# Moving the int8-style quantisation passes of a BitLinear feed-forward from VectorE to ScalarE, with shorter and split scale chains

## The reference

```python
def act_quant(x):
    scale = 127.0 / clip(max(abs(x), axis=-1), 1e-05)
    return clip(round(x * scale), -128, 127) / scale
def bitlinear(x, w, b):                       # weights ternary, w = q * s
    return einsum('bsd,fd->bsf', act_quant(rmsnorm(x)), weight_quant(w)) + b
h = layernorm(x) * (1 + cb) + sb
x = x + gb * bitlinear(gelu(bitlinear(h, w1, b1)), w2, b2)   # 1024 -> 4096 -> 1024
```

## Time and profile before

| | |
|---|---|
| time, median of 3 runs | 6217.45 us (6212.48 to 6218.86) |
| profiled execution, time | 6216.62 us |
| its span, slowest core | 6215.1 us (cores 6200.4 to 6215.1) |
| busy: PE, DVE, ACT | 2608.1, 3996.5, 1913.1 us |
| mean granted TensorE clock | 0.685 |

### The profile page before, as it was taken

One profiled execution on the slowest core, in us unless ns is written; L12 is line 12 of the kernel. 1 busy time (PEld: TensorE's weight loads), 2 busy tenths in 40 slices (PEclk: granted clock), 3 DMA queues, 4 the chain that ended last, 5 costly groups with the idle time before them and its releaser, 6 DMA issues.

```text
span 6215.1 us, 49470 instructions; the slowest of 8 cores (6200.4 to 6215.1 us)
## 1 busy us (share of the span) xinstructions
PE 2608.1 (42%) x12096; PEld 1374.9 (22%) x12096; DVE 3996.5 (64%) x9950; ACT 1913.1 (31%) x3579; POOL 26.2 (0%) x53
## 2 busy tenths in 40 slices
PE   5612342333333234233333323200057777777777
PEld 5501221221122122122112212100023333323333
DVE  0027557566656755756665675478887777777775
ACT  0004345335334434533533443300022222222222
POOL 0000000000000000000000000010000000000000
PEclk9995565665665566566566556555578888888888
DMA  2130000000000000000000000240000000000000
GB/s 86 78 80 1 14 14 1 14 14 1 14 14 14 1 14 14 1 14 14 1 14 14 14 0 7 58 70 0 0 7 21 21 21 21 21 21 21 21 21 14
DMA packets 31716, 123.15 MB, mean 20 GB/s; under 512 B 4756, under 2 KB 6565, under 8 KB 29382
## 3 DMA queue, kind: packets, MB, share of 16 engines
q1 hardware_dynamic: 24486, 98.95, 4.5%
q0 software_dynamic: 6944, 21.05, 2.1%
HBM read 106.95 MB, written 34.08 MB: 23 GB/s over the span
## 4 chain that ended last, share of the span: by engine, by line
DVE 47%; PE 16%; DVEq 11%; DMA 7%; ACT 7%; issue 7%; ACTq 3%; SPq 1%; POOL 0%; POOLq 0%
PE psY L41 8%; DVEq L324 7%; DVE are_bf L1012 6%; DVE zz L875 5%; PE psZ L41 4%; DVE aim_bf L1018 4%; ACTq L324 3%; PE psMC L41 3%; DVE nbuf L979 2%; ACT sin_bf L988 2%; DVE bnst L1477 2%; DMA x_sb<-xmid 2%; DVE aim_bf L1003 2%; DVE wstage L1536 2%; DMA wmstg<-wmod 1%
## 5 line engine op out<-in xcount | busy, mean ns | idle before, releaser
L41 PE MATMUL psZ<-pw_sb,sel_sb 32*128 32x256 f32 x256 | 146.6, 686 | 1322.3 <-DVEq L324 852.1
L41 PE MATMUL psY<-w1q,q1f 128*128 128x512 bf16 x2048 | 566.2, 427 | 1.9 <-ACTq L324 1.7
L41 PE MATMUL psY<-w2q,q2f 128*128 128x512 bf16 x2048 | 460.3, 380 | 2.9 <-ACTq L324 2.9
L41 PE MATMUL psZ<-hbf,win 128*128 128x256 bf16 (+1 forms) x2176 | 309.7, 303 | 241.6 <-ACTq L324 239.4
L41 PE MATMUL psY<-are_bf,bd_sb 128*128 128x256 bf16 x512 | 130.8, 409 | 654.1 <-ACTq L324 644.2
L1012 DVE TENSOR_TENSOR_SCAN are_bf<-are_bf,ncar_re 128x256 bf16<-128x256 bf16 x512 | 374.5, 731 | 16.4 <-issue 1.4
L41 PEld LDWEIGHTS psZ<-pw_sb,sel_sb 32*128 32x128 f32 x256 | 66.2, 309 | 1380.5 <-issue 1377.5
L1018 DVE TENSOR_TENSOR_SCAN aim_bf<-aim_bf,ncar_im 128x256 bf16<-128x256 bf16 x512 | 371.2, 725 | 0.0
L1000 DVE TENSOR_TENSOR are_bf<-cos_bf,g_bf 128x256 bf16<-128x256 bf16 x512 | 146.1, 285 | 294.8 <-ACTq L324 278.6
L875 DVE SCALAR_TENSOR_TENSOR zz<-z,wcv_sb,zz 128x256 f32<-128x256 f32 (+1 forms) x816 | 326.7, 478 | 5.9
L1457 ACT ACTIVATE h_act<-psY,al 128x512 bf16<-128x512 f32 x256 | 175.9, 687 | 491.5 <-PE psY L41 357.7
(11 more groups left out here) (222 smaller groups left out, 5630.4 us busy)
## 6 DMA issues: line engine op xcount, KB each, us to landing
wmstg<-wmod SPq DMA_DIRECT2D x8, 3072.0 KB, 11.1
x_sb<-x SPq DMA_DIRECT2D x32, 512.0 KB, 5.9
xmid<-xo_sb SPq DMA_DIRECT2D x32, 512.0 KB, 3.2
x_sb<-xmid SPq DMA_DIRECT2D x32, 512.0 KB, 4.0
out<-xo_sb SPq DMA_DIRECT2D x32, 512.0 KB, 2.9
w1q<-w1T POOLq DMA_DIRECT2D x8, 1024.0 KB, 24.0
w2q<-w2T POOLq DMA_DIRECT2D x32, 256.0 KB, 5.7
win<-in_proj_w POOLq DMA_DIRECT2D x8, 520.0 KB, 6.2
```

Of the source, the lines that this page charges most:

```text
L41: r = _a(*args, **kw)
```

## The change

The q1 and q2h passes go from DVE to ACT, as two `activation` calls of the function Copy each, with the scale and the magic constant as scale and bias; the copy to f32 in q2h goes away. The quantisation scale is now 127 / max directly, without the inverse square root, so it can be had before qrsqrt. cs1 becomes **cs1b**, behind q1 in the program and with the qrsqrt that stood at the end of h2. st2 and cs2 become **cs2a** (four one-column operations, before q2h) and **cs2b** (the rest, behind q2h in the program, with four one-column operations in place of nine after the qrsqrt).

```diff
@@ front @@
-                    qrsqrt(e, c2, 8, 6)
+                    e.tensor_scalar(out=col(c2, 10), in0=col(c2, 7),
+                                    scalar1=1e-6, scalar2=None, op0=ALU.max)
+                    e.drain()
+                    e.reciprocal(out=col(c2, 10), in_=col(c2, 10))
+                    e.drain()
+                    e.tensor_scalar(out=col(c2, 11), in0=col(c2, 10),
+                                    scalar1=127.0, scalar2=None, op0=ALU.mult)
                 b.stage("vector", s_h2, ...
-                def s_cs1(e, c2=c2):
+                def s_q1(e, c2=c2):
+                    e.activation(out=h2_sb[:], in_=h2_sb[:], func=AF.Copy,
+                                 scale=col(c2, 11), bias=MAGIC)
+                    e.drain()
+                    e.activation(out=q1_bf[:], in_=h2_sb[:], func=AF.Copy,
+                                 bias=-MAGIC)
+                b.stage("scalar", s_q1, reads=("h2", cn),
+                        writes=("q1", "h2"))
+                def s_cs1b(e, c2=c2):
+                    qrsqrt(e, c2, 8, 6)
                     e.tensor_tensor(out=col(c2, 9), in0=col(c2, 7),
                                     in1=col(c2, 8), op=ALU.mult)
...
+                    e.tensor_scalar(out=al1[u8][:, 0:1], in0=col(c2, 9),
+                                    scalar1=col(smallc, 0),
+                                    scalar2=1.0 / 127.0, ...)
+                    e.reciprocal(out=col(c2, 14), in_=al1[u8][:, 0:1])
+                b.stage("vector", s_cs1b, reads=(cn, "smallc"),
+                        writes=(cn, f"al1_{u8}", f"iac1{up}"))
-                def s_q1(e, c2=c2, up=up):
-                    e.tensor_scalar(...); e.tensor_scalar(...)
-                b.stage("vector", s_q1, reads=("h2", cn),
-                        writes=("q1", "h2"))
@@ back @@
-                b.stage("vector", s_st2, reads=("bnst2", "amx"), writes=(cn,))
-                b.stage("vector", s_cs2, reads=(cn, "smallc"),
-                        writes=(cn, f"al2_{u8}", f"iac2{up}"))
+                b.stage("vector", s_cs2a, reads=("amx",), writes=(cn,))
                 for hh in range(8):
                     def s_q2h(e, c2=c2, hh=hh):
-                        e.tensor_copy(out=wstage[:], in_=h_act[:, hs:hs + 512])
+                        e.activation(out=wstage[:], in_=h_act[:, hs:hs + 512],
+                                     func=AF.Copy, scale=col(c2, 11),
+                                     bias=MAGIC)
                         e.drain()
-                        e.tensor_scalar(... col(c2, 11), MAGIC, mult, add)
-                        e.drain()
-                        e.tensor_scalar(out=h_act[:, hs:hs + 512], ... subtract)
-                    b.stage("vector", s_q2h, reads=(f"ha{hh}", cn),
+                        e.activation(out=h_act[:, hs:hs + 512], in_=wstage[:],
+                                     func=AF.Copy, bias=-MAGIC)
+                    b.stage("scalar", s_q2h, reads=(f"ha{hh}", cn),
                             writes=(f"ha{hh}", "wstage"))
+                def s_cs2b(e, c2=c2):      # bn_aggr, mean square, qrsqrt, al2, iacol2
+                b.stage("vector", s_cs2b, reads=(cn, "smallc", "bnst2"),
+                        writes=(cn, f"al2_{u8}", f"iac2{up}"))
```

More of the change, by code:

```diff
@@ L1375, in s_cs1 @@
                     e.drain()
-                    e.tensor_scalar(out=col(c2, 9), in0=col(c2, 9),
-                                    scalar1=1e-5, scalar2=None, op0=ALU.max)
+                    e.tensor_scalar(out=al1[u8][:, 0:1], in0=col(c2, 9),
+                                    scalar1=col(smallc, 0),
+                                    scalar2=1.0 / 127.0,
+                                    op0=ALU.mult, op1=ALU.mult)
                     e.drain()
-                    e.reciprocal(out=col(c2, 10), in_=col(c2, 9))
@@ L1483, in p2_back, with s_cs2a, s_q2h @@
                             writes=("bnst2", "amx"))
-                def s_st2(e, c2=c2):
+                def s_cs2a(e, c2=c2):
                     e.reduce_max(out=col(c2, 7), in_=amx[:, 0:8], axis=AX)
+                    e.drain()
+                    e.tensor_scalar(out=col(c2, 10), in0=col(c2, 7),
+                                    scalar1=1e-6, scalar2=None, op0=ALU.max)
+                    e.drain()
+                    e.reciprocal(out=col(c2, 10), in_=col(c2, 10))
+                    e.drain()
+                    e.tensor_scalar(out=col(c2, 11), in0=col(c2, 10),
+                                    scalar1=127.0, scalar2=None, op0=ALU.mult)
+                b.stage("vector", s_cs2a, reads=("amx",), writes=(cn,))
+                for hh in range(8):
+                    def s_q2h(e, c2=c2, hh=hh):
+                        hs = hh * 512
+                        e.activation(out=wstage[:], in_=h_act[:, hs:hs + 512],
+                                     func=AF.Copy, scale=col(c2, 11),
+                                     bias=MAGIC)
+                        e.drain()
+                        e.activation(out=h_act[:, hs:hs + 512], in_=wstage[:],
+                                     func=AF.Copy, bias=-MAGIC)
+                    b.stage("scalar", s_q2h, reads=(f"ha{hh}", cn),
+                            writes=(f"ha{hh}", "wstage"))
+                def s_cs2b(e, c2=c2):
                     e.bn_aggr(out=c2[:, 17:19], in_=bnst2[:, 0:48])
@@ L1504, in s_cs2 @@
                     e.drain()
-                    e.tensor_scalar(out=col(c2, 9), in0=col(c2, 9),
-                                    scalar1=1e-5, scalar2=None, op0=ALU.max)
+                    e.tensor_scalar(out=al2[u8][:, 0:1], in0=col(c2, 9),
+                                    scalar1=col(smallc, 2),
+                                    scalar2=1.0 / 127.0,
+                                    op0=ALU.mult, op1=ALU.mult)
                     e.drain()
-                    e.reciprocal(out=col(c2, 10), in_=col(c2, 9))
@@ L1509, in s_cs2 @@
[L1509 to L1525, removed]
+                    e.reciprocal(out=col(c2, 14), in_=al2[u8][:, 0:1])
                     e.drain()
                     e.tensor_copy(out=iacol2[up][:], in_=col(c2, 14))
-                b.stage("vector", s_cs2, reads=(cn, "smallc"),
+                b.stage("vector", s_cs2b, reads=(cn, "smallc", "bnst2"),
@@ L1529, in p2_back @@
                         writes=(cn, f"al2_{u8}", f"iac2{up}"))
-                for hh in range(8):
-                    def s_q2h(e, c2=c2, hh=hh):
-                        hs = hh * 512
-                        e.tensor_copy(out=wstage[:], in_=h_act[:, hs:hs + 512])
[L1535 to L1542, removed]
-                    b.stage("vector", s_q2h, reads=(f"ha{hh}", cn),
-                            writes=(f"ha{hh}", "wstage"))
```

13 lines of the change are left out of this document (removed).

## The result

The kernel after takes 6481.16 us (6478.02 to 6485.77), the kernel before, on the same chip, 6217.3 (6212.48 to 6219.41). The ratio is 1.0425, with an interval of 1.0414 to 1.0437. The forecast was 6494, with a range of 6360 to 6570. The profiled execution took 6483.32 us with a span of 6481.4 on its slowest core.

The account below looks back on a forecast made before the run. DVE's 49.4 us and a wait bound the kernel before; after, the chain from C (end of a unit's last w1mm) to w2mm_0. Terms +11, -2.5, +232, +20.4, +9.1, +6.9 make +277 on 6215.1, with 1.5 around it 6494 us; range 6360 to 6570.

Parts of the forecast that it names:

- DVE does not bound the cycle after: Phase 2 unit cycle: DVE, with 33 us left, bounds nothing by its sum; the chain C to w2mm_0 remains.
- The sign given for it: Profile after: DVE busy under 3.5 ms would show the forecast right.
- The 16.5 us: DVE work removed per unit: q2h 13.2 us, q1 1.65, and seven one-column operations of 0.23 each.
- cs2b behind the last q2h: On DVE, cs2b starts only after the last q2h, as it writes c2; its column reaches ia2t at C+26.0.
- The order of stages: Planner's order: ACT runs q2h 0, tq1e, q2h 1 to 7, q1, ia2e; DVE runs ln2 before stats 5 to 7.
- the rival: Second rival, DVE behind C: ln2 does not delay the stats, cs2a 4.2 us earlier for 29 cycles, 6372 us; 8 in 100.
- q2h on ACT: Between cs2a and cs2b: eight q2h take 12.3 us, 1.54 each; bounds 8.3 and 12.8.
- w2mm_0 at a low clock: Start of w2mm_0 on PE: 8.67 us in place of 7.07, 1.6 more; 0 to 3.2 possible.
- The sum: Whole run, C(u) ending unit u's last w1mm: 27 cycles at +8.6, other terms, together +277 on 6215.1.
- The start: Ahead of C(0), unit 0's last w1mm end: h2(1) and ln2(2) slip between weight reductions on DVE, +11 us.
- The first one: Freed engine sets the pace: cycle falls to PE's sum, about 5840 us, if w2mm_0 starts before C+22.7; 5 in 100.
- The third rival: On DVE, h2(u+3) goes between ln2 and stats 6, delaying cs2a 7.7 us for 28 cycles, about 6710; 7 in 100.

Follow-up runs that it names:

- e1: Kernel after with q1 and q2h put back on DVE in their old form, new scale chains and stage order kept: 6475.07 us, ratio 1.0398.
- e4: Kernel after with cs2a's columns in a buffer of their own, so cs2b no longer waits for q2h: 6403.44 us, ratio 1.0285.
- e5: Kernel after with ln2 tied behind cs2a: 6367.43 us, ratio 1.0238.
- e8: e6 with ln2 tied behind cs2a and q2h tied behind tq1e: 6167.27 us, ratio 0.9914.
- e9: e8 with cs2b, ia2t and ia2e moved to the second half, so w2mm_0 does not wait for the row: 6064.93 us, ratio 0.9759.
- e6: e4 with cs2b, ia2t and ia2e ahead of q2h, and q2h in pairs ahead of their transposes: 6257.72 us, ratio 1.0064.
- e3: Kernel before with only the back changed (cs2a, q2h on ACT, cs2b); old front kept: 6700.05 us, ratio 1.0763.
- e11: e9 with q1 and all q2h passes back on DVE: 6105.33 us, ratio 0.9814.
- e10: e9 with q2h of chunks 4 to 7 tied behind the copies tq2e_0 and tq2e_1 of the same unit: 6035.86 us, ratio 0.9707.
- e2: Kernel before with only the front changed (q1 on ACT, cs1b); old st2, cs2 and q2h kept: 6181.64 us, ratio 0.9923.
- e7: Kernel after with the first pass of every q2h done twice: 6681.47 us, ratio 1.074.
- e12: e10 with q1 tied behind the same copies too: 6047.36 us, ratio 0.9721.

## Why the prediction was right, point by point

- **DVE does not bound the cycle after.** Right. It is busy 27.4 us in 59.7, and e1 with 15 us more on it is no slower. The sign given for it, DVE busy under 3.5 ms, was missed: 3.59 ms. The 16.5 us were time with the gaps between instructions, and the busy time that left DVE is 12.6 us a unit. The count was wrong too: cs2a gains three one-column operations, as h2 does, so four leave and not seven. DVE's instructions fell from 9950 to 8990, 30 a unit: 24 of q2h, 2 of q1 and these four. With that the 16.5 would be 15.8. None of it enters the time.
- **cs2b behind the last q2h.** Right as a row: it starts at C+21.4, with 13.96 us of waiting put down to ACT. e4 shows what it costs by itself, 78 us of the 264. My text didn't say what comes late next when this wait goes, and e4's expectation was 31 us too low for that.
- **The order of stages.** Right on all three engines, q2h 0, tq1e, q2h 1 to 7, q1, ia2e among them. ln2 stands ahead of the last three stats; e5 prices this at 114 us where the rival had 122.
- **q2h on ACT.** 12.3 us had been taken from the nearest rows, and the eight take 12.2: 721 and 629 ns a pass where 687 and 620 stood. The two forms differ by 92 ns, and q1's two passes of 1024 columns by 91 (1147 and 1056). The difference in form is the scale from a column, besides the types. By the Trainium skill (ScalarE: Activation LUTs, What ACT_TABLE_LOAD costs) such an operand adds about 93 ns, and the groups above agree.
- **w2mm_0.** Predicted at C+31.3, found at C+30.8: the last q2h ends 0.2 earlier, cs2b to ia2t is 0.1 and the rest of the way 0.2 shorter.
- **w2mm_0 at a low clock.** All w2 matmuls are busy 512.5 us against 460.3 before, 1.6 us a unit, the 1.6 of the prediction. The value was copied from unit 31, so it fits by luck as well; the cycle shown has 7.96, 0.9 more than before, and others more.
- **The sum.** The term of the cycle was mis-sized: +7.9 measured where +8.6 stood, 27 times, 19 us too much. C(28) to C(30) is 116.1 (117.5), C(30) to C(31) 56.9 (56.6), and unit 31's rest 6.4 more than before (6.9).
- **The start.** C(0) is 20.7 us later, where the prediction had 11. C(0) to C(1) is 2.4 shorter (2.5). Two rows tell the parts of the 20.7. The first ln2 on DVE, right behind phase 1, starts at 4007.40 against 4000.18, which the change doesn't touch, and which is another core and another execution. The rest is 13.5, where h2(1) and ln2(2) were to cost 11: they did slip between the weight reductions, and the next step, L1248, is 18.8 later than before, 11.6 without those 7.2. What the last 1.9 are is open. The errors of start and cycle have opposite signs, so the time is nearer (13 us) than its terms.

```profile
4290.08 0.81 DVE L1341 TENSOR_SCALAR h_sb<-x_sb,c 128x1024 f32<-128x1024 f32 x1 [0.19 <-issue]
...
4307.42 0.69 DVE L1328 BATCH_NORM_STATS2 bnst<-x_sb 128x6 f32<-128x512 f32 x1 [0.19 <-issue]
```

- **The rivals.** The first one's condition was a w2mm_0 before C+22.7, and e8 and e9 meet it: with C+19.4 and C+16.7 they are faster than before, e6 with C+25.3 is slower. Its time, 5840, supposed a cycle of about 40, PE's sum, and was never near: in e9 PE is busy 38.8 of the 46.9 us, and 7.8 us of waits are left between C and w2mm_0. The third rival's order is e3's.

## What to carry to other kernels

When work moves off the busiest engine, draw the chain between the two points where the scarce engine waits, and put each moved stage, and each stage that now shares a buffer or a queue with it, in its place there; the busy shares of all engines can look better while the chain grows. A buffer that holds a value needed early and one computed late ties the two together; giving the early one its own buffer, and moving what only the second half needs out of the first, was worth more here than the change of engine. And price such ties from the front of the chain: ln2's tie, the first in it, gave its 3.8 us in full (e5), while the buffer's, further back, brought ia2t 13.8 us forward and w2mm_0 only 2.4 (e4), as the next stages in the queue took over the wait.

## What the runs showed of the hardware

The gains of e8 and e9 were 77 and 70 us smaller than the chain gave, and w2mm_0 is where they went. Windows of e9 (columns as in rows 1), from C to w2mm_0, w2mm_0, and the rest:

```profile
5365.40:5382.00 16.60, 8.81 (x52) 4.27 (x53) 8.07 (x37) 13.92 (x39) 0.00 (x0) 0.82 0.00 0
5382.10:5391.00 8.90, 8.90 (x32) 3.45 (x31) 4.29 (x15) 5.72 (x8) 0.00 (x0) 0.76 0.00 1
5391.10:5412.20 21.10, 20.90 (x95) 8.35 (x96) 14.79 (x27) 6.63 (x22) 0.00 (x0) 1.00 0.16 51
```

And of e11, whose w2mm_0 takes 7.07, the same first two stretches:

```profile
5334.10:5353.10 19.00, 7.77 (x44) 3.68 (x43) 15.09 (x42) 6.04 (x27) 0.00 (x0) 0.73 0.16 56
5353.20:5360.20 7.00, 7.00 (x33) 3.04 (x33) 5.74 (x15) 0.69 (x1) 0.00 (x0) 1.00 0.01 2
```

In e9 the granted clock is 0.82 before w2mm_0 and 0.76 in it, so partly at the lower of its levels of 1.2 and 2.4 GHz; in e11 it is 0.73 before and 1.00 in it. Over all units the w2 matmuls are busy 531.1 us in e10 against 460.3 before, 2.2 us a unit. Thirty-two times that is the 70 us that e9 missed (its own busy time, 520.4 us, comes from 2015 recorded matmuls of 2048; over all it would be 529).

It would be easy to read this as the price of a shorter stretch between C and w2mm_0. The other kernels rule that out. The start and time of w2mm_0 in the cycles read, and the mean of the w2 matmuls over all units:

| kernel | w2mm_0 starts at C+ (us) | w2mm_0 (us) | mean w2 matmul (ns) |
|---|---|---|---|
| before | 24.3 | 7.07 | 380 |
| e2 | 23.0 | 7.07 | 385 |
| e11 | 19.1 | 7.07 | 382 |
| e9 | 16.7 | 8.95 | 420 |
| e8 | 19.4 | 9.99 | 421 |
| e4 | 28.4 | 8.73 | 419 |
| after | 30.8 | 7.96 | 411 |
| e1 | 31.0 | 8.82 | 412 |
| e7 | 36.8 | 9.47 | 412 |

Short and long stretches alike go with a slow w2mm_0. It is fast where the q2h passes are on DVE and the transposes follow them chunk by chunk (before, e2, e11), and slow in most units where one or both are missing; e1, with the passes on DVE, is slow. What PE did just before differs: in e11 its last wait, 9.95 us, ends at 5346.10, and it works without a gap for the 7 us up to w2mm_0, while in e9 waits of 3.83 and 1.09 us stand in the last 6. But in e12 a w2mm_0 right behind a wait of about 3 us takes 7.07 in some cycles and 8.75 in others of the same core. What decides the level was not tested apart and stays open. For a forecast it matters that w2mm_0 took 0.9 to 2.9 us more than its old 7.07 in all the slow rows of the table: a chain of waits priced at the old durations promised too much.
